# VectorE adds the finished row sums at the head of each slot

## The chip, the cores and the metric

The kernel is one program on one core of a Trainium2 chip. The metric is the device time of one execution in microseconds (us): the median of the runs shown, lower is better. The core has four compute engines with a queue of instructions each, executed in order and tied to each other by semaphores: TensorE (PE, matrix products and transposes, with the loads of its weights as PEld), VectorE (DVE), ScalarE (ACT) and GpSimd (POOL), and SyncE (SP), which starts transfers.

## What is computed

A graph layer with a state-space branch, then a mixture of experts, over 6250 nodes of 256 features and 200000 edges sorted by target. The part around the change:

```
proj = x @ gat_w.T;  s_src, s_tgt = sums of proj * a_src, a_tgt per head
e     = leaky_relu(s_src[src] + s_tgt[tgt]);  exp_e = exp(e - shift)
denom = segment_sum(exp_e, tgt);  agg = segment_sum(proj[src] * exp_e, tgt)
perm  = argsort(degree + noise)                 # "ranking"
dA = exp(dt * A);  dBx = dt * xc * B            # per channel, 16 states
h_t = dA_t * h_(t-1) + dBx_t;  y_t = h_t @ C_t  # scan over 6250 rows of x[perm]
```

What follows (gate, feed-forward, experts) is not touched.

## The kernel before

Edges are worked off in 440 "pairs" of one block of up to 512 edges and one tile of 128 target nodes. A pair takes four steps spread over the engines. GpSimd gathers its 512 table rows (L498). VectorE forms the logits of four pairs at once (L516 to L533, five small steps) and multiplies three quarters of the rows by their weights (`scale`, L541); ScalarE does the last quarter (`scale_last`, L584). TensorE multiplies the rows by a one-hot matrix, eight matmuls into the one PSUM tile `fl_ps` (`gather_sums`, L626). VectorE adds that tile to the sums in SBUF, `ACC` (`add`, L551). Since there is one tile `fl_ps`, `gather_sums` of a pair waits until the pair before it is added, and `add` of a pair waits until its own `gather_sums` is done. The one-hot matrix is made on ScalarE (L559, L565), turned on TensorE (L601) and copied on ScalarE (L573); `spread` (L613) gives the logits their target scores.

The pairs are spread over other work, by hand and one per slot: 36 beside the count of degrees, 56 beside ranking, 12 beside the scatter of rows into sorted order, and 336 in the main loop, which does the scan. In slot S, VectorE adds pair S-3, scales pair S-1 and, every fourth pair, forms logits; TensorE does `gather_sums` of pair S-2, then turns and spreads pair S+4.

The main loop has 28 chunks of 224 rows, each with 16 slots, one per state; call them beats 0 to 15 of a chunk. Beats 0, 4, 8 and 12 have no pair, the other twelve have one; the logits fall on beats 1, 6 and 11. In the slot of beat M, in queue order:

- VectorE: `read_out(M-1)` (the product with C, L1068, which lets TensorE reuse the PSUM tile of the copies), two scans (L1059), `add(S-3)`, `scale(S-1)`, some of the next chunk's preparation (L1076 to L1107, beats 7, 8, 10, 11, 12), `inflow(M+1)` (L1048, which reads TensorE's copies of beat M+1). In beat 1 `give_out` (L1118, L1121) comes first. Logit steps, where there are some, stand between these.
- TensorE: `copies(M+1)` (L1288, waits for `read_out(M-1)`), `sum_up(M-1)` (L1298), `gather_sums(S-2)` (L626, waits for `add(S-3)`), turn, spread, then the next chunk's products: beat 2 z (L1304), beat 4 the convolution (L1329), beat 6 (L1335), beat 8 (L1342), beat 10 the output product (L1304).

The place of the add now, with `steps` the logits' generator:

```
read_out(M - 1) ... next(steps); scan(M, 0); next(steps); scan(M, 1); next(steps)
if S:
    add(dve, S - 3)
...
scale(dve, S - 1); prepare(c + 1, 1 - b, at); inflow(M + 1)
```

In ranking and in the scatter, `edges_vector` does three logit steps, the add, two logit steps and the scale; in the count the add already stands first. `add` begins with a register load of the tile's number, from which the address in `ACC` is made.

Of the kernel before, what the change touches and what calls it, by code (L numbers as in the profile page):

```python
# [30 lines left out]
GU = 4  # L31
# [420 lines left out]
def streams(nc, sem, w, a, dram, srcT, parts, tile_of):  # L452
# [19 lines left out]
    with ExitStack() as ctx:  # L472
# [36 lines left out]
        def logits(dve, p):  # L509

            q, n = p.number, p.n
            g, grp = n // GU % 2, p.of(GU)
            dve.wait_ge(s["spread"], q + GU)
            for u in range(GU):
                dve.wait_ge(gathered[g * GU + u], p.of(2 * GU) * 16 * NJ + 16 * NJ)
            nc.vector.tensor_reduce(S8[:], pX[:, :, 0:6 * NH].rearrange("p c (s v) -> p c v s", v=2 * NH), AX_X, ALU.add  # L516
                                    ).then_inc(s["logit"], 1)
            yield
            dve.wait_ge(s["logit"], grp * 5 + 1)
            nc.vector.tensor_tensor(Z[:], G[g][:, :, D:], S8[:, :, 0:NH], ALU.add).then_inc(s["logit"], 1)  # L520
            yield
            dve.wait_ge(s["logit"], grp * 5 + 2)
            nc.vector.scalar_tensor_tensor(L[:], Z[:], 0.2, Z[:], ALU.mult, ALU.max).then_inc(s["logit"], 1)
            yield
            dve.wait_ge(s["logit"], grp * 5 + 3)

            nc.vector.tensor_tensor(DM[:], L[:], S8[:, :, NH:], ALU.subtract).then_inc(s["logit"], 1)
            nc.vector.scalar_tensor_tensor(Q[:], pX[:, :, 6 * NH:].to_broadcast([P, GU * NJ, NH]), -BIG, L[:], ALU.add,
                                           ALU.add).then_inc(s["logit"], 1)
            yield  # L530
            dve.wait_ge(s["logit"], grp * 5 + 5)
            nc.vector.tensor_scalar(DM[:], DM[:], 0.0, None, ALU.min).then_inc(s["shifted"], 1)
            nc.vector.tensor_tensor(EM[:], EM[:], Q[:], ALU.max)  # L533
            yield

        def scale(dve, p):
            q, n = p.number, p.n
            g, at = n // GU % 2, slice(n % GU * NJ, (n % GU + 1) * NJ - 1)
            dve.wait_ge(s["weight"], p.of(GU) + 1)
            rows = G[g][:, at, 0:D].rearrange("p j (h f) -> p j h f", h=NH)  # L540
            nc.vector.tensor_tensor(rows, rows, weight[:, at, :].unsqueeze(3).to_broadcast([P, NJ - 1, NH, FO]),  # L541
                                    ALU.mult).then_inc(s["scaled"], 1)

        def add(dve, p):
            q = p.number
            k = dve.value_load(tile_of[0:1, bass.ds(q, 1)], min_val=0, max_val=NT - 1)
            at = ACC[:, bass.ds(k, 1), :].rearrange("p o d -> p (o d)")
            if not early(q, 1):
                dve.wait_ge(s["added"], q)
            dve.wait_ge(s["summed"], q + 1)  # L550
            nc.vector.tensor_tensor(at, at, pS, ALU.add).then_inc(s["added"], 1)  # L551
# [76 lines left out]
            mm.then_inc(s["summed"], 1)  # L628

        def edges_vector(dve, S):  # L630
            steps = logits(dve, S) if S.n % GU == 0 else None
            if steps:
                next(steps)
                next(steps)
                next(steps)
            add(dve, S - 3)
            if steps:
                next(steps)
                next(steps)
            scale(dve, S - 1)  # L640

        def edges_scalar(act, S):
# [135 lines left out]
        with ExitStack() as part:  # L778
# [34 lines left out]
            def _(dve):  # L813
# [24 lines left out]
                for q in range(G_COUNT, G_RANK):  # L838
                    if q == first:
                        dve.wait_ge(loaded, 32)  # L840
                        dve.wait_ge(turned_k, 1)
                        done(nc.vector.tensor_copy(KC[:], pK[:]))
                    edges_vector(dve, pair(q))
                    if first <= q < first + NT:
                        compare(q - first)
# [36 lines left out]
        with ExitStack() as part:  # L882
# [138 lines left out]
            def _(dve):  # L1021
# [19 lines left out]
                def inflow(p):  # L1041

                    m, n = p.number, p.n
                    dve.wait_ge(s["BC"], m + 1)
                    if not early(m, 2):

                        dve.wait_ge(s["h"], (m - 1) * KD)
                    nc.vector.tensor_tensor(dB[:, n % 2], U[:, n // NS % 2], pBC[n % 2][:, 0, :].unsqueeze(1).to_broadcast([P, KD, TC]),  # L1048
                                            ALU.mult).then_inc(s["dB"], 1)

                def scan(p, k):
                    m, n = p.number, p.n
                    if k == 0:
                        dve.wait_ge(s["dB"], m + 1)
                        dve.wait_ge(s["dA"], m + 1)
                        if not early(m, 2):

                            dve.wait_ge(s["h0"], m - 1)
                    nc.vector.tensor_tensor_scan(H[:, n % 2, k, :], dA[:, n % 4, k, :], dB[:, n % 2, k, :],  # L1059
                                                 H0[:, k, n % NS:n % NS + 1], ALU.mult, ALU.add).then_inc(s["h"], 1)  # L1060

                def read_out(p):
                    m, n = p.number, p.n
                    dve.wait_ge(s["h"], (m + 1) * KD)
                    if not early(m, 2):

                        dve.wait_ge(s["y"], m - 1)
                    nc.vector.tensor_tensor(HC[:, n % 2], H[:, n % 2], pBC[n % 2][:, 1, :].unsqueeze(1).to_broadcast([P, KD, TC]),  # L1068
                                            ALU.mult).then_inc(s["hc"], 1)
# [41 lines left out]
                def give_out(c, b):  # L1111

                    dve.wait_ge(s["y"], (c + 1) * NS)
                    if not early(c, 1):

                        dve.wait_ge(s["o"], c)
                    for k in range(KD):
                        nc.vector.scalar_tensor_tensor(Y[:, k, :], XC[:, b, k, :], DP[:, k:k + 1], pY[:, k, :], ALU.mult,  # L1118
                                                       ALU.add).then_inc(s["skip"], 1)
                    dve.wait_ge(s["skip"], (c + 1) * KD)  # L1120
                    nc.vector.tensor_tensor(Y[:], Y[:], SZ[:, b], ALU.mult).then_inc(s["gated"], 1)  # L1121

                def slot(M, S):
                    n, c = M.n, M.of(NS)
                    at, b = n % NS, n // NS % 2
                    if at == 1 and not early(c, 1):
                        give_out(c - 1, 1 - b)
                    if not early(M.number, 1):
                        read_out(M - 1)
                    steps = logits(dve, S) if S and S.n % GU == 0 else None  # L1130
                    if steps:
                        next(steps)
                    scan(M, 0)
                    if steps:
                        next(steps)
                    scan(M, 1)
                    if steps:
                        next(steps)
                    if S:
                        add(dve, S - 3)  # L1140
                    if steps:
                        next(steps)
                        next(steps)
                    if S:
                        scale(dve, S - 1)
                    prepare(c + 1, 1 - b, at)
                    inflow(M + 1)

                for k in range(SCAT):
                    edges_vector(dve, pair(G_RANK + k))  # L1150
                for k in range(PREP):
                    edges_vector(dve, pair(G_RANK + SCAT + k))
                    for at in range(k * NS // PREP, (k + 1) * NS // PREP):
                        prepare(0, 0, at)
                inflow(Slot(0, 0))
                run(dve, slot)
                read_out(Slot(0, SLOTS - 1))
                add(dve, pair(PAIRS - 3))
# [1076 lines left out]
```

## Time and profile before

| | before |
|---|---|
| median of 3 runs | 3993.34 us (3987.35 to 3993.79) |
| the profiled execution, its own time | 3986.44 us |
| its span, first to last instruction | 3984.8 us |
| mean granted TensorE clock | 0.875 of full |
| busy: PE, DVE, ACT, POOL | 74%, 69%, 59%, 62% of the span |
| main loop | about 986 to 3034 us |

Times in the profile are microseconds from the first instruction. A line of the timeline is: start, duration, engine, source line, operation, tile written <- tiles read, count, and in brackets how long the engine sat idle before it and what released it. Rows that follow each other on one engine may overlap a little, since instructions are pipelined. "issue" is a wait for nothing that the profile shows.

### The profile page before, as it was taken

Reading aid. Unit: us, or ns where it says so; the run is one execution under the profiler, and the core shown is the slowest. Engines: PE = TensorE matmul, PEld = TensorE weight load, DVE = VectorE, ACT = ScalarE, POOL = GpSimd, SP = SyncE. Lnnn points to the kernel's source line nnn. Section 1 sums busy time; section 2 is a strip of 40 time slices with the busy share of each in tenths; the row PEclk is TensorE's granted clock in tenths of the full one; section 3 lists DMA queues with packets and bytes.
Section 4 is the critical chain, followed back from the end, with each engine's and each line's share of the span. In section 5 each row is a group of like instructions: output and inputs, shape, how many; then the busy total and the mean of one; then the engine's idle time right before and its main releaser. Section 6 shows DMA issues by size and latency. Waiting matters only on the chain. (4 is left out here: it accounts for less than half of the span.)

```text
span 3984.8 us, 66165 instructions
## 1 busy us (share of the span) xinstructions
PE 2963.8 (74%) x16306; PEld 2207.7 (55%) x16307; DVE 2733.2 (69%) x5474; ACT 2350.2 (59%) x5989; POOL 2475.2 (62%) x2259
## 2 busy tenths in 40 slices
PE   5355556645888878878888888788784888749998
PEld 4245445533656556556556555565562455438887
DVE  4466668953888888888888888888885688611111
ACT  2133344424887877877877877878783565512222
POOL 4488765676766766766766666666665376424443
PEclk8678777766999989998989999999997999969999
DMA  4333354455444444444444444444447233237675
GB/s 154 101 90 87 85 141 101 115 156 144 119 118 120 116 114 113 118 115 115 119 115 112 119 117 112 116 118 113 120 112 150 56 92 93 87 115 143 143 144 106
DMA packets 284702, 460.40 MB, mean 116 GB/s; under 512 B 57719, under 2 KB 203624, under 8 KB 284168
## 3 DMA queue, kind: packets, MB, share of 16 engines
q0 software_dynamic: 121472, 292.57, 30.6%
q1 hardware_dynamic: 162952, 165.07, 14.8%
q14 instruction: 220, 1.80, 0.1%
q8 instruction: 58, 0.95, 0.1%
HBM read 394.01 MB, written 63.44 MB: 115 GB/s over the span
## 5 line engine op out<-in xcount | busy, mean ns | idle before, releaser
L498 POOL DMA_INDIRECT el_g<-table,el_ix x1344 | 1377.8, 1025 | 661.0 <-issue 380.2
L626 PE MATMUL fl_ps<-el_g,el_oh 128*128 128x260 f32 x3520 | 1032.5, 444 | 319.3 <-DVE ACC L551 315.1
L626 PEld LDWEIGHTS fl_ps<-el_g,el_oh 128*128 128x128 f32 x3520 | 746.4, 220 | 647.7 <-issue 502.9
L498 POOL DMA_INDIRECT el_g<-table,eg_src x436 | 531.8, 1220 | 229.2 <-issue 128.6
L1059 DVE TENSOR_TENSOR_SCAN mb_h<-mb_dA,mb_h,mb_dB 128x224 f32<-128x224 f32 x896 | 569.5, 668 | 24.4 <-ACT mb_dA L1186 14.4
L565 ACT ACTIVATE el_oht<-el_away 128x512 bf16<-128x512 bf16 x445 | 280.3, 630 | 330.1 <-PE fl_px L613 315.7
L584 ACT ACTIVATE el_g<-el_g 128x64 f32<-128x64 f32 x1760 | 463.3, 336 | 0.0
L1298 PE MATMUL fl_py<-mb_hc,ident 128*128 128x448 f32 x896 | 432.4, 565 | 0.0
L541 DVE TENSOR_TENSOR el_g<-el_g,fl_pw 128x768 f32<-128x768 f32 x440 | 416.1, 946 | 0.0
L559 ACT ACTIVATE el_away<-el_dst,el_less 128x512 bf16<-128x512 bf16 x445 | 319.3, 717 | 152.3 <-DMA el_dst<-dst_rows 62.6
L1186 ACT ACTIVATE mb_dA<-mb_dt,mb_a 128x224 f32<-128x224 f32 x900 | 383.4, 475 | 1.4
L1048 DVE TENSOR_TENSOR mb_dB<-mb_u,fl_pbc 128x448 f32<-128x448 f32 x449 | 275.0, 612 | 130.6 <-PE fl_pbc L1288 128.7
L2176 POOL DMA_INDIRECT out<-ex_y,ex_to x112 | 174.1, 1554 | 279.5 <-DVE ex_y L2135 254.9
L1288 PE MATMUL fl_pbc<-mb_parts,mb_sel 96*128 96x224 bf16 x898 | 165.5, 267 | 203.9 <-DVE mb_hc L1068 202.3
L1068 DVE TENSOR_TENSOR mb_hc<-mb_h,fl_pbc 128x448 f32<-128x448 f32 x448 | 274.1, 612 | 18.0 <-issue 18.0
L551 DVE TENSOR_TENSOR ACC<-ACC,fl_ps 128x260 f32 x440 | 181.5, 412 | 129.9 <-PE fl_ps L626 97.1
L2135 DVE TENSOR_TENSOR ex_y<-ex_py,ex_b 128x512 f32<-128x512 f32 x56 | 38.8, 692 | 333.4 <-PE ex_py L2097 333.4
L601 PE MATMUL fl_pt<-el_ident,el_oht 128*128 128x128 bf16 x1776 | 187.2, 233 | 100.8 <-ACT el_oh L573 83.9
L601 PEld LDWEIGHTS fl_pt<-el_ident,el_oht 128*128 128x128 bf16 x1776 | 147.4, 106 | 192.3 <-ACT el_oht L565 97.4
L573 ACT CAST el_oh<-fl_pt 128x512 f32<-128x512 bf16 x443 | 251.7, 568 | 0.7
L2150 ACT COPY ex_xt<-ex_px 128x512 f32<-128x512 f32 x56 | 32.8, 585 | 345.8 <-PE ex_px L2071 345.8
L2086 PE MATMUL ex_ph<-ex_xt,ex_w 128*128 128x256 f32 x896 | 205.3, 383 | 1.8 <-DMA ex_b<-in_moe_b 1.1
(303 smaller groups left out, 5193.1 us busy)
## 6 DMA issues: line engine op xcount, KB each, us to landing
el_dst<-dst_rows SPq DMA_DIRECT2D x446, 128.0 KB, 3.5
ex_w<-in_moe_W SPq DMA_DIRECT2D x56, 512.0 KB, 3.6
el_g<-table,el_ix POOLq DMA_INDIRECT x1344
ex_x<-routed_x SPq DMA_DIRECT2D x56, 257.0 KB, 2.7
el_g<-table,eg_src POOLq DMA_INDIRECT x436
mb_x<-sorted_x SPq DMA_DIRECT2D x30, 224.0 KB, 3.2
table<-px_tr POOLq DMA_DIRECT2D x49, 130.0 KB, 2.4
px_x<-in_x SPq DMA_DIRECT2D x49, 128.0 KB, 3.4
```

Source lines behind the costliest of these rows:

```text
L498: pool.indirect_dma_start(out=G[b // GU][:, b % GU * NJ + j, :], out_offset=None, in_=dram["table"], in_offset=bass.IndirectOffsetOnAxis(a ...
L541: nc.vector.tensor_tensor(rows, rows, weight[:, at, :].unsqueeze(3).to_broadcast([P, NJ - 1, NH, FO]), ALU.mult).then_inc(s["scaled"], 1)
L559: nc.scalar.activation(AWAY[:], DST[:, n % 4, :], ACT.Abs, bias=LESS[:, 0:1]).then_inc(s["away"], 1)
L565: nc.scalar.activation(OHT[:, n % 2, :], AWAY[:], ACT.Relu, bias=1.0, scale=-1.0).then_inc(s["hot"], 1)
L584: ins = nc.scalar.activation(row[:, h * FO:(h + 1) * FO], row[:, h * FO:(h + 1) * FO], ACT.Identity, scale=row[:, D + h:D + h + 1])
L601: mm = nc.tensor.transpose(pT[:, j, :], OHT[:, n % 2, j * P:(j + 1) * P], I16[:])
L626: mm = nc.tensor.matmul(pS, OH[:, n % (2 * GU), j, :], G[n // GU % 2][:, n % GU * NJ + j, :], start=j == 0, stop=j == NJ - 1)
L1048: nc.vector.tensor_tensor(dB[:, n % 2], U[:, n // NS % 2], pBC[n % 2][:, 0, :].unsqueeze(1).to_broadcast([P, KD, TC]), ALU.mult).then_inc( ...
L1059: nc.vector.tensor_tensor_scan(H[:, n % 2, k, :], dA[:, n % 4, k, :], dB[:, n % 2, k, :], H0[:, k, n % NS:n % NS + 1], ALU.mult, ALU.add). ...
L1068: nc.vector.tensor_tensor(HC[:, n % 2], H[:, n % 2], pBC[n % 2][:, 1, :].unsqueeze(1).to_broadcast([P, KD, TC]), ALU.mult).then_inc(s["hc" ...
L1186: ins = nc.scalar.activation(dA[:, n % 4, k, :], DT[:, n // NS % 2, k, :], ACT.Exp, scale=A[:, k, n % NS:n % NS + 1])
L1298: nc.tensor.matmul(pY[:], w["ident"][:], HC[:, n % 2], start=n % NS == 0, stop=n % NS == NS - 1).then_inc(s["y"], 1)
```

## The change

In the main loop `add(S-3)` moves from behind the two scans to the head of the slot, ahead of `read_out(M-1)` (in beat 1 behind `give_out`). In `edges_vector`, used in ranking and in the scatter, it moves ahead of the logits' first three steps; in the slots without logits the order there stays as it is. No instruction is added or taken out.

```diff
         def edges_vector(dve, S):
-            steps = logits(dve, S) if S.n % GU == 0 else None
-            if steps:
-                next(steps)
-                next(steps)
-                next(steps)
             add(dve, S - 3)
-            if steps:
-                next(steps)
-                next(steps)
+            if S.n % GU == 0:
+                for _ in logits(dve, S):
+                    pass
             scale(dve, S - 1)
...
                     if at == 1 and not early(c, 1):
                         give_out(c - 1, 1 - b)
+                    if S:
+                        add(dve, S - 3)
                     if not early(M.number, 1):
                         read_out(M - 1)
                     steps = logits(dve, S) if S and S.n % GU == 0 else None
...
                     scan(M, 1)
                     if steps:
                         next(steps)
-                    if S:
-                        add(dve, S - 3)
-                    if steps:
                         next(steps)
                         next(steps)
```

## Rows read from the trace of the kernel before

**Rows 1.** Engines' busy time in ranking, in the scatter, and in the main loop (columns in the first line).

```profile
core 0: us, PE busy (x) PEld busy (x) DVE busy (x) ACT busy (x) POOL busy (x), PEclk, DMA share, GB/s
496.00:848.00 352.00, 220.75 (x2074) 179.61 (x2074) 289.35 (x517) 157.19 (x420) 215.38 (x225) 0.72 0.45 121
848.00:986.00 138.00, 53.58 (x252) 40.93 (x252) 39.35 (x68) 46.33 (x112) 100.39 (x97) 0.66 0.54 159
986.00:3034.00 2048.00, 1667.31 (x8958) 1204.87 (x8958) 1741.06 (x3472) 1652.54 (x4424) 1385.47 (x1374) 0.93 0.46 116
```

**Rows 2.** Two waits of the main loop: us in total, times, longest us.

```profile
PE fl_pbc L1288 <- DVE mb_hc L1068: 202.3, 107, 4.4
PE fl_ps L626 <- DVE ACC L551: 127.7, 150, 2.2
```

**Rows 3.** Timeline of VectorE, beats 13 to 15 of one chunk.

```profile
2063.76 0.61 DVE L1068 TENSOR_TENSOR mb_hc<-mb_h,fl_pbc 128x448 f32<-128x448 f32 x1
...
2067.18 0.61 DVE L1068 TENSOR_TENSOR mb_hc<-mb_h,fl_pbc 128x448 f32<-128x448 f32 x1
...
2069.64 0.42 DVE L551 TENSOR_TENSOR ACC<-ACC,fl_ps 128x260 f32 x1 [0.69 <-PE fl_ps L626]
2069.99 0.94 DVE L541 TENSOR_TENSOR el_g<-el_g,fl_pw 128x768 f32<-128x768 f32 x1
...
2071.38 0.61 DVE L1068 TENSOR_TENSOR mb_hc<-mb_h,fl_pbc 128x448 f32<-128x448 f32 x1
```

**Rows 4.** Timeline of TensorE over the same beats, to the head of beat 0.

```profile
2064.43 0.36 PE L1288 MATMUL fl_pbc<-mb_parts,mb_sel 96*128 96x224 bf16 x2 [3.79 <-DVE mb_hc L1068]
...
2066.01 3.41 PE L626 MATMUL fl_ps<-el_g,el_oh 128*128 128x260 f32 x8 [0.44 <-DVE ACC L551]
...
2069.59 0.35 PE L1288 MATMUL fl_pbc<-mb_parts,mb_sel 96*128 96x224 bf16 x2
...
2070.55 1.92 PE L626 MATMUL fl_ps<-el_g,el_oh 128*128 128x260 f32 x8
...
2072.63 0.35 PE L1288 MATMUL fl_pbc<-mb_parts,mb_sel 96*128 96x224 bf16 x2
...
2075.78 0.35 PE L1288 MATMUL fl_pbc<-mb_parts,mb_sel 96*128 96x224 bf16 x2
```

**Rows 5.** Timeline of VectorE, beats 1 and 2 (logits in beat 1).

```profile
2083.51 0.61 DVE L1068 TENSOR_TENSOR mb_hc<-mb_h,fl_pbc 128x448 f32<-128x448 f32 x1
```

**Rows 6.** Timeline of TensorE, beat 1.

```profile
2081.71 3.80 PE L626 MATMUL fl_ps<-el_g,el_oh 128*128 128x260 f32 x8 [0.62 <-DVE ACC L551]
```

**Rows 7.** Timeline of VectorE, beats 6 and 7 (logits in beat 6).

```profile
2101.53 0.61 DVE L1068 TENSOR_TENSOR mb_hc<-mb_h,fl_pbc 128x448 f32<-128x448 f32 x1
2104.12 0.56 DVE L516 TENSOR_REDUCE el_s<-fl_px 128x128 f32<-128x384 f32 x1 [1.98 <-PE fl_px L613]
...
2106.36 0.43 DVE L551 TENSOR_TENSOR ACC<-ACC,fl_ps 128x260 f32 x1 [0.26 <-issue]
...
2108.73 0.61 DVE L1068 TENSOR_TENSOR mb_hc<-mb_h,fl_pbc 128x448 f32<-128x448 f32 x1
```

**Rows 8.** Timeline of TensorE, beat 6.

```profile
2103.64 0.35 PE L1288 MATMUL fl_pbc<-mb_parts,mb_sel 96*128 96x224 bf16 x2
...
2106.93 1.99 PE L626 MATMUL fl_ps<-el_g,el_oh 128*128 128x260 f32 x8 [2.17 <-DVE ACC L551]
```

**Rows 9.** Timeline, beat 9's product on TensorE and beat 10's read-out on VectorE.

```profile
2117.77 1.99 PE L626 MATMUL fl_ps<-el_g,el_oh 128*128 128x260 f32 x8 [0.44 <-DVE ACC L551]
...
2118.93 0.61 DVE L1068 TENSOR_TENSOR mb_hc<-mb_h,fl_pbc 128x448 f32<-128x448 f32 x1
```

**Rows 10.** Timeline of VectorE, one ranking slot with logits.

```profile
650.94 0.56 DVE L516 TENSOR_REDUCE el_s<-fl_px 128x128 f32<-128x384 f32 x1 [1.78 <-PE fl_px L613]
...
652.61 0.42 DVE L551 TENSOR_TENSOR ACC<-ACC,fl_ps 128x260 f32 x1 [0.59 <-issue]
```

**Rows 11.** A wait of the add in ranking, 496 to 848 us.

```profile
DVE ACC L551 <- issue: 8.3, 14, 0.6
```

## The prediction, made before the changed kernel ran

> **What bounds the kernel now.** I read the stages' busy times first. The main loop is 2048 of 3985 us, and there no engine is full: TensorE is busy 1667 us, VectorE 1741, ScalarE 1653 [rows 1]. So its pace is set by how the queues wait for each other, beat by beat. The waits say where: TensorE waits 202 us in 107 beats for the read-out, which frees the tile of its copies, and 128 us in 150 beats for the add [rows 2]. The change shortens the second and, since the add now stands ahead of the read-out, can lengthen the first.
>
> The timelines decide which. A chunk repeats 28 times, 2048 / 28 = 73.1 us each. In beats 14 and 15 TensorE runs without a gap: from copies to copies 3.04 us (2069.59 to 2072.63) and 3.15 us (to 2075.78) [rows 4]. It can, because VectorE is ahead: its read-out of beat 14 starts at 2067.18, while the product of the beat before, begun at 2066.01, takes 3.41 us and ends at 2069.42; VectorE does read-out and both scans in that time and only then waits, 0.69 us, for the sums [rows 3, 4]. The same lead stands in beat 2 (read-out 2083.51, product of beat 1 ends 2081.71 + 3.80 = 2085.51 [rows 5, 6]), in beat 6 (read-out 2101.53, TensorE is through with beat 5 at 2103.64 [rows 7, 8]) and in beat 10 (2118.93 against 2117.77 + 1.99 = 2119.76 [rows 9]). With the add at the head that lead is forbidden: the add waits for the product of the beat before, and read-out, scans, scale and inflow are queued behind it; TensorE's next copies wait for that read-out, and ScalarE's copy of the last state for the scans.
>
> **The cost of a locked beat.** From the start of a fast product: 1.92 us to its end [rows 4]; 0.22 until the add starts (2069.42 to 2069.64); 0.35 until VectorE takes the next instruction (2069.64 to 2069.99) [rows 3]; 0.67 from the read-out's start to the copies (2063.76 to 2064.43) [rows 3, 4]; 0.96 from the copies over sum_up to the next product (2069.59 to 2070.55) [rows 4]. Together 4.12 us, of which I take 4.05, since the semaphore comes a little before the modelled end. Against 3.04 to 3.15 us now that is about +1.0 us. It is paid only where a pair stands in the beat before as well (beats 2, 3, 6, 7, 10, 11, 14, 15); in beats 1, 5, 9 and 13 the product was two beats ago and the add waits for nothing.
>
> **The chunk, walked through with these durations** (shift of VectorE's path against now, at the end of the beats named):
> - Beat 1, logits: give_out, then the add without a wait. Now the add starts 0.26 us late for an "issue" wait behind the third logit step (so in beat 6, [rows 7]); that is gone, -0.2. TensorE's product no longer waits 0.62 us [rows 6], but its copies start 0.34 us later.
> - Beats 2 and 3 are locked: VectorE +1.4. TensorE has its own z product to do in beat 2, so its copies are only 0.5 us later.
> - Beats 4 and 5: VectorE has slack under the convolution, and only TensorE's +0.5 is left.
> - Beat 6, locked and with logits: copies at 2105.1 instead of 2103.64, +1.5. But the product now waits for the add until 2106.93, 2.17 us [rows 8]; with the add in front it starts 0.96 after the copies, 2106.1, 0.8 earlier. The two nearly cancel by beat 7: VectorE +0.3, TensorE 0.
> - Beats 7 to 9 are paced by VectorE, whose work is only reordered: still +0.3. In beat 9 the add ahead of the read-out delays the copies 0.34 us, while the product's wait of 0.44 us goes [rows 9].
> - Beat 10, locked: the read-out starts at 2120.2 instead of 2118.93; +1.0 on VectorE after its own preparation. Beat 11, logits: -0.5. Left: +0.5.
> - Beats 12 and 13 are VectorE's (preparation; TensorE idles 3.79 us before beat 13 [rows 4]): +0.5.
> - Beats 14 and 15, locked, with nothing of TensorE's to hide it: copies +1.3 in 14, +2.3 in 15; VectorE ends the chunk at +2.5.
>
> The next chunk starts with give_out, which waits on VectorE's path, so 2.5 us is the price of a chunk: 27.5 x 2.5 = **+69 us** (the first chunk has no give_out). Bounds from the same rows: at worst all eight locked beats cost 1.0 us with nothing given back, 28 x 8 = +224 us; at best each of the three logit beats saves VectorE 0.26 us and nothing locks, -22 us. The walk stands nearer the lower end because in five of the eight other work covers the wait.
>
> **Ranking.** Only 14 of 56 slots change, those with logits. Each has 0.59 us of issue wait before the add (8.3 us in 14 times [rows 10, 11]): the add's register load starts once the third step is released. At the head it lies under the comparison before it. In the slot shown VectorE also waits 1.78 us for the spread before its first step [rows 10], and the add's 0.35 us fits in there: -0.9. VectorE is busy 289 of 352 us here [rows 1], so it passes on: 14 slots by 0.6 to 0.9 is -8 to -13; I take **-12**, with the first slots, where TensorE sets the pace and gets its product almost 2 us earlier, at the upper end. Nothing can be lost: the add's product is done before the spread that the logits wait for, as TensorE's queue has it in that order.
>
> **Scatter.** 3 logit slots in 138 us in which VectorE is busy 39 us [rows 1]; transfers set its end. 0 to -3; I take **-2**.
>
> No transfer, weight load or instruction is added. GpSimd's gathers wait for a product eight pairs back, so they follow the pace. The count's order stays.
>
> Sum: 69 - 12 - 2 = +55 us on the profiled execution's 3986.4 us, 4041. That execution lies 7 us below the median of the runs; against the median it is 3993.3 + 55 = 4048. I forecast between them, **4045 us**.
>
> **The clock.** In the main loop 0.93 of full clock is granted, so TensorE is at its lower level (1.2 instead of 2.4 GHz) for some 14% of it, 287 us or 10 us a chunk [rows 1]; a product then takes 3.80 instead of 1.92 us [rows 4, 6], and before the low stretch in beat 14's rows it idled 3.79 us. I take that as unchanged: the gaps of the locked beats are 0.9 us, those of beats 1 and 13 stay. If a third of the low time went or came, 3.4 us a chunk at half speed, it would be 1.7 x 28 = 48 us either way. The Trainium skill, page "TensorE: Matmul & The Clock Gate", part 1, has it that the engine is throttled by default and activity releases the throttle; by it a change that removes 2.17 us waits for the add could raise the clock. That is the second rival.
>
> **Rivals.** About 0.2%, 8 us, is what a measurement of this kernel can tell from no change.
> 1. The forecast, head wait locks the queues: slower, around 4045, its own range 4010 to 4095. For it: the lead in four places of the rows. Chance 0.71.
> 2. The clock gains from the waits that go: 55 - 48 = +7, about 4000. Against: as much idle time is added in other beats. Chance 0.10, half of it within 0.2%.
> 3. Other side: the product of the beat before ends before VectorE reaches the head, in beats 2, 3, 6, 10, 14 and 15. TensorE starts that product earlier when it does not wait for the add; if it gains more than the lead VectorE has now (0.8 us in beat 10, 2.0 in beat 2), nothing locks. Then only savings are left: -22 in the main loop, -12, -2 = -36, about 3955. It decides at a lead of zero. For it: the 128 us of waits for the add [rows 2]. Against: in beats 14 and 15 TensorE does not wait at all now, so it can gain nothing there. Chance 0.12.
> 4. The locks also push ScalarE, whose one-hot matrices TensorE needs: one more locked beat a chunk not covered, +28 to +55: 4070 to 4100. Chance 0.07.
>
> Slower by over 0.2%: 0.71 + 0.07 and a third of rival 2, 0.81. Within: 0.06. Faster: 0.13. The range leaves out rival 3 and the top: 3990 to 4100.
>
> **What would show it.** In the changed profile, the add waiting for the product should grow from few and short to some six beats a chunk, and the read-out follow it by 0.35 us; copies to copies in beats 14 and 15 about 4.05 us; TensorE's wait for the add close to nil, its wait for the read-out up by more than the 128 us; the chunk 2.5 us longer; ranking 12 us shorter, without the 0.59 us issue waits. I am wrong if copies to copies in beats 14 and 15 stays near 3.1 us, or if the granted clock of the main loop moves from 0.93 by more than 0.03.

## The result, and the profile after

The changed kernel takes 4054.4 us (median of 4 runs, 4048.33 to 4064.42) against 3993.57 us: ratio 1.0157, 95% interval 1.0144 to 1.0171, or 63 us slower by the ratio (60.8 by the two medians; the differences of the runs below go by their ratios, times 3992 us). The forecast was 4045 us, 55 us slower.

The page of the changed kernel. Lines 551 to 626 keep their meaning; the read-out is now L1063, the scan L1054, the copies L1282, sum_up L1292. Columns: busy us, mean ns, then idle time before the group and its releaser.

```profile
span 4046.7 us, 66163 instructions
...
PE 2950.2 (73%) x16306; PEld 2232.5 (55%) x16307; DVE 2735.9 (68%) x5474; ACT 2360.3 (58%) x5989; POOL 2429.6 (60%) x2259
...
L626 PE MATMUL fl_ps<-el_g,el_oh 128*128 128x260 f32 x3520 | 991.9, 432 | 180.1 <-DVE ACC L551 179.9
...
L1282 PE MATMUL fl_pbc<-mb_parts,mb_sel 96*128 96x224 bf16 x898 | 170.9, 274 | 391.6 <-DVE mb_hc L1063 391.3
...
L551 DVE TENSOR_TENSOR ACC<-ACC,fl_ps 128x260 f32 x440 | 185.7, 422 | 332.6 <-PE fl_ps L626 308.8
```

The page of before has for the last two:

```profile
L1288 PE MATMUL fl_pbc<-mb_parts,mb_sel 96*128 96x224 bf16 x898 | 165.5, 267 | 203.9 <-DVE mb_hc L1068 202.3
...
L551 DVE TENSOR_TENSOR ACC<-ACC,fl_ps 128x260 f32 x440 | 181.5, 412 | 129.9 <-PE fl_ps L626 97.1
```

There it was 129.9 us of idle time before the add and 203.9 before the copies; now it is 332.6 and 391.6. The busy times of TensorE, VectorE and ScalarE stayed within 0.5%: nothing costs more, the queues wait longer.

Where, by stage (columns in the first line; answers to [rows 1]):

```profile
core 0: us, PE busy (x) PEld busy (x) DVE busy (x) ACT busy (x) POOL busy (x), PEclk, DMA share, GB/s
496.00:842.00 346.00, 217.25 (x2074) 176.71 (x2074) 289.17 (x517) 157.21 (x420) 215.52 (x225) 0.73 0.46 123
842.00:981.00 139.00, 54.45 (x252) 41.36 (x252) 39.85 (x68) 46.12 (x111) 101.12 (x97) 0.65 0.53 159
981.00:3103.00 2122.00, 1659.86 (x8958) 1234.20 (x8958) 1747.06 (x3472) 1662.03 (x4424) 1334.32 (x1374) 0.91 0.43 112
```

Ranking is 6 us shorter, the scatter 1 us longer, the main loop 2122 instead of 2048 us. From first scan to last the loop took 2038.8 us before (986.1 to 3024.9) and 2113.5 now (981.3 to 3094.8): +74.7. What follows the last scan took 959.9 us and now takes 951.9, though no instruction of it is changed. In the traces of the runs below it takes 954.4 to 959.5 us, whichever place the add has, so it varies by several us by itself; what makes it vary was not tried. The sum is -4.8 + 74.7 - 8.0 = +61.9, the difference of the spans.

The waits of the main loop of the changed kernel (us in total, times, longest; answers to [rows 2]):

```profile
PE fl_pbc L1282 <- DVE mb_hc L1063: 391.3, 293, 5.2
...
DVE ACC L551 <- PE fl_ps L626: 208.2, 169, 3.3
```

TensorE's wait for the read-out grew from 202 to 391 us and from 107 to 293 beats, while its own wait for the add, 128 us before, is no longer among the long ones. VectorE waits 208 us at the add, 169 times, which is six beats a chunk.

The same beats as in [rows 3, 4], first VectorE, beats 13 to 15:

```profile
2097.17 0.61 DVE L1063 TENSOR_TENSOR mb_hc<-mb_h,fl_pbc 128x448 f32<-128x448 f32 x1
...
2103.32 0.43 DVE L551 TENSOR_TENSOR ACC<-ACC,fl_ps 128x260 f32 x1 [2.99 <-PE fl_ps L626]
2103.66 0.61 DVE L1063 TENSOR_TENSOR mb_hc<-mb_h,fl_pbc 128x448 f32<-128x448 f32 x1
...
2107.37 0.43 DVE L551 TENSOR_TENSOR ACC<-ACC,fl_ps 128x260 f32 x1 [0.55 <-PE fl_ps L626]
2107.71 0.61 DVE L1063 TENSOR_TENSOR mb_hc<-mb_h,fl_pbc 128x448 f32<-128x448 f32 x1
```

and TensorE:

```profile
2097.84 0.56 PE L1282 MATMUL fl_pbc<-mb_parts,mb_sel 96*128 96x224 bf16 x2 [3.17 <-DVE mb_hc L1063]
2098.19 1.73 PE L1292 MATMUL fl_py<-mb_hc,ident 128*128 128x448 f32 x2
2099.71 3.39 PE L626 MATMUL fl_ps<-el_g,el_oh 128*128 128x260 f32 x8
...
2104.33 0.36 PE L1282 MATMUL fl_pbc<-mb_parts,mb_sel 96*128 96x224 bf16 x2 [0.92 <-DVE mb_hc L1063]
...
2105.30 1.92 PE L626 MATMUL fl_ps<-el_g,el_oh 128*128 128x260 f32 x8
...
2108.38 0.36 PE L1282 MATMUL fl_pbc<-mb_parts,mb_sel 96*128 96x224 bf16 x2 [0.85 <-DVE mb_hc L1063]
...
2109.35 1.92 PE L626 MATMUL fl_ps<-el_g,el_oh 128*128 128x260 f32 x8
...
2111.46 0.37 PE L1282 MATMUL fl_pbc<-mb_parts,mb_sel 96*128 96x224 bf16 x2
```

The chain is plain to read. The product of beat 13 ends at 2103.10 (2099.71 + 3.39); the add starts at 2103.32, the read-out at 2103.66, the copies at 2104.33. From these copies to the next it is 4.05 us, which is the locked beat as it was costed, against 3.04 before. In the last interval, into beat 0, which has no pair, it is 3.08.

Taken over 26 chunks from the starts of the copies in the trace, the mean from one beat 2 to the next is 73.06 us before and 75.68 after, +2.62 (the walk said +2.5). By beats, mean us from one beat's copies to the next beat's:

| beat | 0 | 1 | 2 | 3 | 4 | 5 | 6 | 7 | 8 | 9 | 10 | 11 | 12 | 13 | 14 | 15 |
|---|---|---|---|---|---|---|---|---|---|---|---|---|---|---|---|---|
| before | 4.32 | 5.98 | 5.05 | 3.04 | 7.01 | 3.04 | 7.18 | 3.24 | 2.44 | 3.80 | 5.59 | 5.33 | 5.03 | 5.24 | 3.05 | 3.72 |
| after | 5.25 | 5.82 | 4.65 | 3.04 | 7.01 | 4.04 | 4.95 | 3.70 | 3.10 | 4.05 | 4.98 | 5.43 | 5.57 | 6.33 | 4.06 | 3.70 |

Beat 5 loses 1.0 us and beat 6 gives back 2.2, because its product no longer waits behind logits and scans; from beat 12 to beat 0 the loss stays.

### The profile page after: what moved, and what is told of

Read it like the earlier page. It is cut to its first block and busy times, and to the rows that moved or that the text cites. A ratio compares the mean times of both kernels' runs of the same rounds, so it can differ in the third digit from the quotient of the medians.

```text
span 4046.7 us, 66163 instructions
## 1 busy us (share of the span) xinstructions
PE 2950.2 (73%) x16306; PEld 2232.5 (55%) x16307; DVE 2735.9 (68%) x5474; ACT 2360.3 (58%) x5989; POOL 2429.6 (60%) x2259
## 5 line engine op out<-in xcount | busy, mean ns | idle before, releaser
L498 POOL DMA_INDIRECT el_g<-table,el_ix x1344 | 1325.9, 987 | 784.5 <-PE fl_ps L626 397.8
L626 PE MATMUL fl_ps<-el_g,el_oh 128*128 128x260 f32 x3520 | 991.9, 432 | 180.1 <-DVE ACC L551 179.9
L626 PEld LDWEIGHTS fl_ps<-el_g,el_oh 128*128 128x128 f32 x3520 | 758.2, 218 | 447.2 <-issue 334.6
L1054 DVE TENSOR_TENSOR_SCAN mb_h<-mb_dA,mb_h,mb_dB 128x224 f32<-128x224 f32 x896 | 569.1, 668 | 24.7 <-issue 23.6
L1292 PE MATMUL fl_py<-mb_hc,ident 128*128 128x448 f32 x896 | 458.9, 597 | 0.0
L1282 PE MATMUL fl_pbc<-mb_parts,mb_sel 96*128 96x224 bf16 x898 | 170.9, 274 | 391.6 <-DVE mb_hc L1063 391.3
L551 DVE TENSOR_TENSOR ACC<-ACC,fl_ps 128x260 f32 x440 | 185.7, 422 | 332.6 <-PE fl_ps L626 308.8
L1282 PEld LDWEIGHTS fl_pbc<-mb_parts,mb_sel 96*128 96x128 bf16 x898 | 59.0, 98 | 454.6 <-DVE mb_hc L1063 444.0
L1063 DVE TENSOR_TENSOR mb_hc<-mb_h,fl_pbc 128x448 f32<-128x448 f32 x448 | 274.2, 612 | 14.6 <-issue 14.6
```

What stands on the lines that cost most here:

```text
L498: pool.indirect_dma_start(out=G[b // GU][:, b % GU * NJ + j, :], out_offset=None, in_=dram["table"], in_offset=bass.IndirectOffsetOnAxis(a ...
L626: mm = nc.tensor.matmul(pS, OH[:, n % (2 * GU), j, :], G[n // GU % 2][:, n % GU * NJ + j, :], start=j == 0, stop=j == NJ - 1)
L1292: nc.tensor.matmul(pY[:], w["ident"][:], HC[:, n % 2], start=n % NS == 0, stop=n % NS == NS - 1).then_inc(s["y"], 1)
```

## The experiments

Two theories stood at first. The lock: what costs is that the add waits at the head for the product of the beat before, with the read-out behind it. The order: what costs is 0.35 us of add ahead of each read-out, waiting or not. A third, the clock, came in with the first runs.

**1. The main loop's edit alone.**

```diff
+                    if S:
+                        add(dve, S - 3)
                     if not early(M.number, 1):
                         read_out(M - 1)
...
-                    if S:
-                        add(dve, S - 3)
```

> The kernel before with the main loop's edit alone (add at the head of the slot, ahead of the read-out); ranking and scatter as before. Theory, the lock (the add at the head waits for the product of the beat before, and the read-out that TensorE's next copies need is queued behind it): the whole loss is here, +66 to +77 us on the kernel before, 4060 to 4070, some 6 us more than the changed kernel. Rival, the clock (more of the main loop at 1.2 GHz, other stages too): less than the whole, +30 to +60.

Measured 4073.89 us, ratio 1.0213 (1.0193 to 1.0233), +85 us. Its loop from first to last scan takes 2116.8 us, 78 more than before and 3 more than in the changed kernel. So the whole loss is the main loop's edit, and the other edit took something off it. The loss lies above the 66 to 77 us expected.

**2. The edit of ranking and scatter alone.**

```diff
-            steps = logits(dve, S) if S.n % GU == 0 else None
-            if steps:
-                next(steps)
-                next(steps)
-                next(steps)
             add(dve, S - 3)
...
+            if S.n % GU == 0:
+                for _ in logits(dve, S):
+                    pass
```

> The kernel before with the edit of the 17 logit slots of ranking and scatter alone. The walk of the prediction says -12 - 2 = -14 us; the two traces say that the first scan of the main loop starts 4.8 us earlier. Expected -3 to -14 us, 3980 to 3991. If ranking's end is set by something else than VectorE (TensorE's counts, transfers), it is nearer to 0.

Measured 3978.6 us, ratio 0.9966 (0.9953 to 0.9979), -14 us: the prediction's -12 - 2. The 4.8 us between the first two traces were too few because this start varies: in the traces of kernels with the old order and one tile of sums the first scan begins at 986.1, 994.4, 994.4, 993.3, 991.7, 994.3 and 995.3 us, in those with the new one at 981.3, 982.9, 982.9 and 983.2, some 10 us earlier on the mean.

**3. The head in the four beats that have nothing to wait for** (1, 5, 9, 13), the old place elsewhere.

```diff
+                    if S and at in (1, 5, 9, 13):
+                        add(dve, S - 3)
                     if not early(M.number, 1):
                         read_out(M - 1)
...
-                    if S:
+                    if S and at not in (1, 5, 9, 13):
                         add(dve, S - 3)
```

> The kernel before with the add at the head only in beats 1, 5, 9 and 13, where no pair stands in the beat before, so that it waits for nothing; elsewhere behind the scans. The lock theory: no loss, the copies come 0.34 us later but the product's wait for the add goes, -8 to +8 us. Rival, the order alone (0.35 us of add ahead of every read-out): 4 of 12 beats, a third of the main loop's 70 us, +20 to +25 us.

Measured 3981.17 us, ratio 0.9977 (0.9966 to 0.9989), -9 us. That is a little past the good end of what was expected. Where nothing waits the head is no loss but a small gain. The order by itself is not what costs here.

**4. The head in beats 14 and 15 alone.** 

```diff
+                    if S and at in (14, 15):
+                        add(dve, S - 3)
                     if not early(M.number, 1):
                         read_out(M - 1)
...
-                    if S:
+                    if S and at not in (14, 15):
                         add(dve, S - 3)
```

> The kernel before with the add at the head only in beats 14 and 15. The lock theory: copies to copies in beat 14 goes from 3.05 to 4.05 us and the read-out of beat 15 likewise; nothing of TensorE's hides it, 28 x 2.0 = +56, taken +40 to +60 us. Rival, the order alone: 2 of 12 beats, +12 us.

Measured 4085.27 us, ratio 1.0228 (1.0209 to 1.0247), +91 us. Two locked beats lose as much as all twelve heads together or more, and more than the lock was costed at. Beat 14 took 4.06 us as expected (3.05 before), but beat 1 went from 5.98 to 6.82, beat 6 from 7.18 to 7.81 and beat 13 from 5.24 to 6.26. The full edit does not lose more, because with its head in beat 6 that beat takes 4.95 us instead of 7.81: it gains there about what its other heads lose. The main loop of this kernel, with TensorE's granted clock as the last number but two:

```profile
992.00:3139.00 2147.00, 1720.63 (x8958) 1248.02 (x8958) 1749.10 (x3473) 1655.02 (x4421) 1366.70 (x1371) 0.90 0.43 110
```

At 0.90 the clock is lower than in the kernel before, 0.93 [rows 1]. In the trace's record of the granted clock the loop is at 1.2 GHz for 300 us before, 362 in the changed kernel and 427 here. By beat, us a chunk at 1.2 GHz:

| beat | 0 | 1 | 2 | 6 | 12 | 13 | whole chunk |
|---|---|---|---|---|---|---|---|
| before | 1.40 | 3.52 | 0.20 | 1.97 | 0.05 | 3.47 | 10.76 |
| changed kernel | 1.37 | 3.62 | 0 | 0 | 3.17 | 4.71 | 12.87 |
| head in 14 and 15 | 1.08 | 6.19 | 1.13 | 3.15 | 0 | 3.41 | 15.23 |

**5. The add between read-out and scans.**

```diff
                     if not early(M.number, 1):
                         read_out(M - 1)
+                    if S:
+                        add(dve, S - 3)
...
-                    if S:
-                        add(dve, S - 3)
```

> The kernel before with the main loop's add between the read-out and the first scan (all twelve beats); ranking and scatter as before. The copies are free again, only the scans stand behind the add. The lock theory: in beats 14 and 15 VectorE's loop is scans 1.17, scale 0.87, inflow 0.53, read-out 0.53 and add 0.35, 3.45 us, and the product it waits for is one beat old, so copies to copies stays under 3.5 us instead of 4.05; most of the loss is gone: -15 to +20 us against the kernel before. If the wait itself, wherever it stands in the slot, is what costs, it stays near +70.

Measured 3988.52 us, ratio 0.9993 (0.9983 to 1.0002): no difference. The add still waits, 107 us in 85 beats (between 1000 and 2960 us, where the changed kernel has 190 in 155), but it no longer holds the read-out. Beat 14 takes 3.60 us, where less than 3.5 was expected. So it is the read-out behind the waiting add that makes the loss of the changed kernel. That the wait behind the read-out costs nothing does not follow: run 8 shows a gain in the logit beats that it cancels here.

**6. Two tiles of sums, the add at the head and one pair later.** Each product then has two slots until its add, and the wait at the head is gone.

```diff
-        weight = pW[:, 0:GU * NJ * NH].rearrange("p (c h) -> p c h", h=NH)
+        pS = [pS, pW[:, 0:ROW]]
+        weight = sb("el_weight", [P, GU * NJ * NH])[:, 0:GU * NJ * NH].rearrange("p (c h) -> p c h", h=NH)
...
-            nc.vector.tensor_tensor(at, at, pS, ALU.add).then_inc(s["added"], 1)
+            nc.vector.tensor_tensor(at, at, pS[p.n % 2], ALU.add).then_inc(s["added"], 1)
...
-            if not early(q, 1):
-                pe.wait_ge(s["added"], q)
+            if not early(q, 2):
+                pe.wait_ge(s["added"], q - 1)
...
-                mm = nc.tensor.matmul(pS, OH[:, n % (2 * GU), j, :], G[n // GU % 2][:, n % GU * NJ + j, :],
+                mm = nc.tensor.matmul(pS[n % 2], OH[:, n % (2 * GU), j, :], G[n // GU % 2][:, n % GU * NJ + j, :],
...
-                        add(dve, S - 3)
+                        add(dve, S - 4)
```

> The changed kernel with two PSUM tiles for the sums in turn (the second in the bank of the weights, which go to SBUF) and the add one pair later (pair S-4), so that the add stands at the head but its product is always two slots old. The lock theory: no wait at the head, no loss; the main loop is no longer than before and TensorE waits less: -10 to -60 us against the kernel before. Rival, the order alone: the loss stays, +40 to +60. The scale now reads its weights from SBUF; its duration (0.946 us) may change, and is read off.

Measured 3928.42 us, ratio 0.9847 (0.983 to 0.9863), -61 us, of which 14 are ranking's as in run 2. The same head place, without the wait, is faster than both kernels. The scale takes 0.933 us (median) with its weights in SBUF, 0.946 before.

**7. Two tiles, the add in its old place and of its old pair.** The two tiles of run 6 put into the kernel before; the add's line is not touched (it stands below the scans, for pair S-3):

```diff
-            if not early(q, 1):
-                pe.wait_ge(s["added"], q)
+            if not early(q, 2):
+                pe.wait_ge(s["added"], q - 1)
...
                     scan(M, 1)
...
                     if S:
                         add(dve, S - 3)
```

> The kernel before with the two PSUM tiles of the run above and the add in its old place and of its old pair. The product waits for the add of the slot before only, which is long done, so TensorE's 128 us of waits for the add in the main loop should be near 0, and VectorE keeps its lead. -10 to -60 us, if those waits were on the path; 0 if VectorE's chain sets the beat anyway.

Measured 3973.97 us, ratio 0.996 (0.9946 to 0.9974), -16 us. TensorE's waits for the add are gone from the loop, 128 us of them, and the loop from first to last scan is no shorter (2048.0 us); the 16 us lie ahead of it, where the first scan begins at 964.8 us (986.1 in the kernel before). That does not show that these waits were on nobody's path. Beats 1 and 6 are shorter than before by 0.6 and 1.5 us; beats 7 and 11 are longer by 0.8 and 1.4, and beat 11 is so because the logits wait there for gathered rows (between 1000 and 2960 us; 0.6 us in one beat in the whole kernel before):

```profile
DVE el_s L517 <- DMA el_g<-table,el_ix: 40.4, 16, 3.0
```

What the waits gave in two beats was taken back in two others, over half of it by late rows. Why the rows come late in this kernel and not in those of runs 6 and 12 was not tried.

**8. The add ahead of the logit steps in the three logit beats alone**, with ranking and scatter as changed.

```diff
                     if not early(M.number, 1):
                         read_out(M - 1)
+                    if S and at in (1, 6, 11):
+                        add(dve, S - 3)
...
-                    if S:
+                    if S and at not in (1, 6, 11):
                         add(dve, S - 3)
```

> The kernel before with ranking and scatter changed as in the changed kernel, and in the main loop the add between read-out and first logit step in the three logit beats (1, 6, 11) alone, elsewhere behind the scans. The product no longer waits for logits and scans there (0.6, 2.2 and 0.6 us now), and VectorE loses the 0.26 us issue wait: -10 to -45 us against the kernel before. If VectorE's chain sets the beat, only -5 for ranking and 84 x 0.26 = -22 at most are left.

Measured 3942.51 us, ratio 0.9879 (0.9863 to 0.9896), -48 us, a little past the good end. Of that 14 are ranking's. This is what was of use in the change: the add out from behind the logits, without holding the read-out. Beat 6 takes 5.57 us instead of 7.18. It also bears on run 5. From first to last scan the loop takes 2001.8 us here and 2030.6 in run 5, whose add stands in the same place but in all twelve beats: in the other nine beats the add between read-out and scans costs 29 us. Beat 14 is 3.04 us here and 3.60 there, where the scans stand behind a waiting add.

**9 and 10. The clock.** Matmuls of no use keep TensorE at work where it waits. They write into the PSUM bank of the weights, which go to SBUF as in run 6. Run 9 is the kernel before with them, run 10 the kernel of run 4.

```diff
+                def spin(times):
+                    for _ in range(times):
+                        nc.tensor.matmul(pW[:, 0:448], w["ident"][:], w["iota"][:, 0:448], start=True, stop=True,
+                                         skip_group_check=True)
...
                         sum_up(M - 1)
+                    if at == 6:
+                        spin(2)
...
                     prepare(c + 1, 1 - b, at)
+                    spin({0: 2, 12: 3}.get(at, 0))
```

> The kernel before with matmuls of no use that keep TensorE busy where it waits for VectorE: three at the end of beat 12, two at the end of beat 0, two ahead of beat 6's product, each 128x448, into the bank that the weights leave for SBUF. What the clock is worth in the kernel before: low-clock time in the main loop from 300 us to under 150. If the low clock costs on the path, -10 to -60 us; 0 if VectorE's chain hides it; a loss if they outlast the waits (about 0.76 us each against waits of 3.8, 1.8 and 2.2 us).

> The same matmuls of no use in the kernel whose add stands at the head in beats 14 and 15 alone, which lost 91 us where the lock gave 56. Theory, the excess is the clock (low-clock time of its main loop 427 us, 127 more than before): against the run before this one, which has the same matmuls, only the lock is left, +50 to +65 us. Rival, VectorE's lost lead costs more than the walk gave, clock or no clock: +85 to +95 against that run.

The kernel before with them: 3998.6 us, ratio 1.0016 (1.0006 to 1.0027), +6 us. Time at 1.2 GHz falls from 300 to 147 us and on balance nothing is gained. The kernel with the head in beats 14 and 15: 4010.7 us, ratio 1.004 (1.0028 to 1.0052); the same filling takes 75 us off it and leaves it 12 us behind the filled kernel before. The first expectation had this as its second case: VectorE's chain hides the low clock. By beats that fits most of it, but not all. Beats 13, 0, 1 and 6 gain 3.0 us a chunk; beats 7 to 9 lose 1.2, beats 14 and 15 1.1, and beat 11 0.7, where the logits now wait for gathered rows, 20 of these 22.6 us in beat 11:

```profile
DVE el_s L516 <- DMA el_g<-table,el_ix: 22.6, 14, 2.5
```

Without that wait the clock might have given some 20 us, an estimate from this line, and the filled kernel before is a base that much too slow. The second failed for both theories: not 50 to 65 us are left and not 85 to 95, but 12. With the lock the low clock is most of the loss: the filling takes 75 of 91 us off, far more than the excess of 35 us that I had put down to it. How much the lock alone leaves is open between these 12 us and some 28, an estimate from the waits for gathered rows, which are 22.6 us in the filled kernel before and only 6.5 in this one.

**11. The same in the changed kernel**, at the ends of beats 0 and 12.

```diff
                     prepare(c + 1, 1 - b, at)
+                    spin({0: 2, 12: 3}.get(at, 0))
```

> The same matmuls of no use at the ends of beats 0 and 12 in the changed kernel (none in beat 6, where it has no wait). Its low-clock time in the main loop is 362 us, 62 more than before. If the clock makes up what the walk missed, the distance to the fill run of the kernel before is the lock alone less ranking's gain, +55 +- 10 us, and the kernel is 10 to 60 us faster than the changed kernel; if the clock has no part, it stays near the changed kernel's 4054.

Measured 3989.22 us, ratio 0.9992 (0.9982 to 1.0001) against the kernel before, so 65 us less than the changed kernel, a little over the top of what was expected. Against the filled kernel before (which has two more such matmuls in beat 6, not ranking's 14 us, and the 22.6 us wait for rows) it is not 55 us slower but 9 us faster; there the expectation failed by 64 us, and the wait for rows can be some 20 of them. Its beats 12 and 13 on TensorE:

```profile
2060.83 3.83 PE L1275 MATMUL fl_pw<-iota,ident 128*128 128x448 f32 x6
2064.90 0.36 PE L1287 MATMUL fl_pbc<-mb_parts,mb_sel 96*128 96x224 bf16 x2 [0.24 <-DVE mb_hc L1063]
2065.10 0.93 PE L1297 MATMUL fl_py<-mb_hc,ident 128*128 128x448 f32 x2
2065.87 1.92 PE L626 MATMUL fl_ps<-el_g,el_oh 128*128 128x260 f32 x8
...
2069.02 0.37 PE L1287 MATMUL fl_pbc<-mb_parts,mb_sel 96*128 96x224 bf16 x2 [0.92 <-DVE mb_hc L1063]
...
2069.99 1.92 PE L626 MATMUL fl_ps<-el_g,el_oh 128*128 128x260 f32 x8
...
2073.07 0.37 PE L1287 MATMUL fl_pbc<-mb_parts,mb_sel 96*128 96x224 bf16 x2 [0.85 <-DVE mb_hc L1063]
```

The six rows of spin are three matmuls and end just as the copies of beat 13 may start. sum_up then takes 0.93 instead of 1.73 us, the product 1.92 instead of 3.39, and from these copies to those of beat 14 it is 4.12 us instead of 6.49. Beat 14 still takes 4.05: the lock is there, only without the low clock. The main loop of this kernel:

```profile
983.00:3036.00 2053.00, 1689.64 (x9236) 1233.19 (x9234) 1748.38 (x3475) 1658.14 (x4424) 1371.13 (x1374) 0.98 0.45 115
```

0.98 of full clock is granted, against 0.91; its chunk takes 73.25 us, against 75.68 in the changed kernel and 73.06 before.

**12. Two tiles, the add between read-out and scans.** The edit of run 6 with the add in the place of run 5:

```diff
                     if not early(M.number, 1):
                         read_out(M - 1)
+                    if S:
+                        add(dve, S - 4)
```

> The kernel with two tiles of sums and the add one pair later, with the add between the read-out and the first scan instead of at the head. The add waits for nothing in either place; the copies come 0.35 us earlier than with the add at the head. If the add ahead of the read-out costs anything once the wait is gone, this beats that kernel's 3928 by up to 12 x 0.35 = 4 us a chunk where TensorE waits for the read-out, that is 0 to -40 us; the lock theory alone says equal within 10 us.

Measured 3883.88 us, ratio 0.9729 (0.9712 to 0.9745), -108 us, the fastest of all. A chunk takes 69.45 us, against 70.94 with the head. VectorE runs from slot to slot without a wait in these beats:

```profile
2008.17 0.61 DVE L1064 TENSOR_TENSOR mb_hc<-mb_h,fl_pbc 128x448 f32<-128x448 f32 x1
2008.78 0.42 DVE L552 TENSOR_TENSOR ACC<-ACC,fl_pw 128x260 f32 x1
...
2011.67 0.61 DVE L1064 TENSOR_TENSOR mb_hc<-mb_h,fl_pbc 128x448 f32<-128x448 f32 x1
2012.20 0.41 DVE L552 TENSOR_TENSOR ACC<-ACC,fl_ps 128x260 f32 x1
...
2015.09 0.61 DVE L1064 TENSOR_TENSOR mb_hc<-mb_h,fl_pbc 128x448 f32<-128x448 f32 x1
2015.62 0.41 DVE L552 TENSOR_TENSOR ACC<-ACC,fl_pw 128x260 f32 x1
```

Read-out to read-out is 3.50 and 3.42 us, and the add, of a pair whose product is long done, follows each read-out without a gap. So the order is not free after all: with the wait gone, the add ahead of the read-out still costs 44 us, a little more than the 40 expected at most. How much of that is the 0.35 us itself and how much the clock (1.2 GHz for 311 us of the loop with the head, 201 here) was not tried.

## Why the prediction was right

**The lead and the lock.** Right, with the numbers: the copies of beats 14 and 15 lie 4.05 us apart where 4.05 was costed, the add starts 0.22 us after the modelled end of the slow product (2103.10 to 2103.32) and 0.15 after that of the fast one (2105.30 + 1.92 = 2107.22 to 2107.37), and the read-out follows it by 0.34. These 0.15 instead of 0.22 are the step from the added-up 4.12 to the 4.05 taken; the reason given for it, a semaphore ahead of the modelled end, is not what the rows show. Run 6 takes the wait away and the loss with it, run 5 takes the read-out out from behind the wait and the loss with it. Beats without a wait cost nothing (run 3).

**The walk.** +2.5 us a chunk was said, 2.62 measured; +69 us for the loop, 74.7 from first to last scan. Beat 5 went as it was walked (+1.0 until the copies of beat 6). In the middle the walk was off: beat 6 gave back 2.2 us where 1.5 was walked, and beats 7 to 9 then lost 1.4. Counted from the copies of beat 2 (+0.5 in the walk), those of beat 7 come 1.1 us earlier instead of level and those of beat 10 at +0.2 instead of +1.3. By beats 14 and 15 the two agree again, +1.4 and +2.4 where +1.3 and +2.3 were walked. That these errors cancelled was luck; the price of the last two beats was not.

**Ranking and scatter.** -14 us was said, -14 measured (run 2). The changed kernel's first trace showed 5, for the start of the loop scatters by several us. The add's issue waits of 0.59 us are gone from ranking, as was said; the add waits there for its product 37 us instead of 27.

**The clock.** Here a step was taken too lightly: "I take that as unchanged". The time at 1.2 GHz went from 300 to 362 us in the loop, 0.93 to 0.91. More important is what it is worth. The walk carried the low-clock products of beats 1 and 13 along (3.80 and 3.41 us, at their places in [rows 4, 6]) and priced the lock with them in it; that is in part why the total came out right. But its price of a locked beat, +1.0 us, was that behind a fast product, and it gave the low clock no share of the loss. The runs say that the two belong together. Before, VectorE does read-out and scans while a low-clock product runs, and raising the clock brings nothing on balance (run 9, some 20 us of late rows apart). With the add at the head, read-out and scans wait until that product has ended, its extra 1.5 us are on the path, and raising the clock brings back 65 us (run 11), although the add still waits 137 us in 154 beats. That is nearly all of the loop's loss: from first scan to last it takes 2043.5 us there, 2113.5 in the changed kernel and 2038.8 before. At a high clock the locked beats cost about what the other beats, beat 6 above all, give back. The second rival had the clock gain from the waits that went; in fact the time at 1.2 GHz rose by 62 us, and what the lock did was to expose it. The Trainium skill, page "TensorE: Matmul & The Clock Gate", part 1, says that activity releases the throttle: in beat 12 the trace agrees, 3.8 us of matmuls of no use and the following product takes 1.92 us instead of 3.39.

**The other side.** The third rival, that TensorE ends its product before VectorE comes to the head, did not happen in beats 2, 3, 6, 10, 14 and 15. It was right in what decides: where there is no wait (runs 6 and 12) the new order gains. The fourth, the push on ScalarE, shows but stays small: TensorE's wait for the copied one-hot matrix goes from 18 to 39 us in the loop, and the 4070 us at which that rival begins are not reached.

**Left open.** Why the head in beats 14 and 15 alone costs more than the 56 us of its two locked beats: its low-clock time in beats 1 and 6 (9.3 us a chunk against 5.5 before) goes with it, and filling takes 75 of 91 us off, but what makes the clock fall more often in those beats was not tried. The filled kernel before is a rough base: its beats 11 and 15 take 6.04 and 4.50 us on the mean, 0.7 and 0.8 more than unfilled; beat 11 is the late rows, beat 15 was not explained. The weights' move from PSUM to SBUF is part of runs 6, 7 and 9 to 12 and was never run alone; of its effects only the scale's duration was read (0.933 against 0.946 us). The 8 us after the last scan.

## What to carry to other kernels

Before moving a waiting instruction to the head of a queue, look at what stands behind it, and whether another engine's next step hangs on that; put it behind the instruction that releases the other engine instead. A lead of one engine over another is worth something that no busy time shows: here it let VectorE work beside TensorE's low-clock products, and giving it up cost 63 us although the waits that the change aimed at went away. If a wait at the head is wanted gone, give it another buffer and take the result one step later: together with the place behind the read-out that made 108 us of gain out of 63 of loss (both with ranking's 14 us in them).

## What was not expected

- Low clock on the path or beside it: halving the time at 1.2 GHz (300 to 147 us) is worth nothing on balance in the kernel before (+6 us, with a new wait of 22.6 us for gathered rows in it), and cutting it from 362 to 99 us is worth 65 us in the changed one.
- Two locked beats cost +91 us (1.0209 to 1.0247), as much as the full edit of the loop with its +85 (1.0193 to 1.0233) or more, since the full edit gains 2.2 us a chunk in beat 6.
- 128 us of waits for the add could be removed without the loop getting shorter (2048.0 against 2038.8 us, run 7), because other waits came in their place, 40 us of them for gathered rows.
- The same place of the add costs 29 us in nine beats and gains in the three with logits; together they look like no change (runs 5 and 8).
- A register load behind a short chain leaves VectorE idle 0.26 us in the main loop and 0.59 us in ranking before the add [rows 7, 10]; at the head in beat 13 of the changed kernel it is 0.33 us, the line at 2096.83:

```profile
2096.83 0.42 DVE L551 TENSOR_TENSOR ACC<-ACC,fl_ps 128x260 f32 x1 [0.33 <-issue]
```
